# A context attention with TensorE's order staggered by one batch, late pairs weighted by ScalarE and summed by GpSimd, and two expert blocks that end without GpSimd's drain

## The chip, the cores and the metric

The kernel runs on one core of one Trainium2 chip. The metric is the time of one execution on the device, in microseconds (us); lower is better. Three runs of the kernel before are at hand, and one more with a profile, from which all rows of this text come.

## The reference

Eight sequences of 256 tokens, 256 numbers each (`x`), go through eight sublayers; four of them attend to a context `ctx` of the same shape. Only what the kernel's stages compute is kept here:

```python
x = x + L0_xattn(layernorm(x), ctx, ctx)      # 16 heads of 16      stage a0
x = x + L0_ffn(layernorm(x))                  # 16 experts choose   stage f1
x = x + L1_xattn(layernorm(x), ctx, ctx)      # 16 heads of 64      stage a2
x = x + L1_ffn(layernorm(x))                  # top 2 of 8 experts  stage f3
x = x + L2_xattn(layernorm(x), ctx)           # one head of 256     stage a4
x = x + L2_ffn(layernorm(x))                  # 8-bit weights       stage f5
x = x + L3_xattn(layernorm(x), ctx, ctx)      # 16 heads of 16      stage a6
x = x + L3_ffn(layernorm(x))                  # block quantised     in a6

def L1_ffn(x):       # every token goes to its two best experts; 4096 pairs in all
    probs = sigmoid(x @ router.T); topw, sel = top_k(probs, 2)
    topw = topw / topw.sum(-1)                # the "share" of each of the two
    return sum(topw * expert[sel](x))         # expert: relu(x @ W1)**2 @ W2

def L2_xattn(key, value):
    att = softmax(key @ value.T / sqrt(256))  # 256 x 256 for each sequence
    return att @ value                        # value is the context
```

## The kernel before

The program is seven stages, one after the other, named above. Each is a block: a list of instructions for each of the five engines (TensorE or PE, VectorE or DVE, ScalarE or ACT, GpSimd or POOL, SyncE or SP), run in the order written, with semaphores between the engines. At the end of a block every engine empties its pipeline (a `Drain`), says so on one semaphore, and goes on when all five have. There is no scheduler: the order in which the code is written is the order of the work. Each stage's GpSimd list begins with `clear_last_stage` (L92 to L94), which sets the semaphores of the last stage to zero; it consists of a `Drain` of GpSimd of its own and a clear.

**f1 to a2.** The expert-choice stage ends with four scatters (L1665), DMAs issued by GpSimd that add the last expert's rows into `x_rows` in DRAM. SP waits for the first two and loads the first half of `x` back (L1359, L1360), still in f1; the second half is loaded in a2 (L240 to L242). The first thing on GpSimd in a2 after the clear is the power that gives the first `rstd` of a layernorm (L63), then a 128x2048 copy (L591).

**f3 to a4.** The top-2 stage writes the result of every expert tile with a scatter (L2601) issued by GpSimd into `y_rows`. In a4, SP and ACT first wait until all 39 scatters have landed (L1740, L1885) and then fetch the rows back, 16 DMAs in all (`fetch_pairs`, L2803): for each token its two results, into `pair_out[:, 0]` and `pair_out[:, 1]`.

**Stage a4, `context_attention` (L1701).** `f` and `b` number the eight sequences, here called batches; a batch is two tiles of 128 tokens. The steps of a batch, with the code's names:

- DVE `take`: x += share0 * pair0 + share1 * pair1, four instructions of 128x256 (L1809)
- DVE `stats`, POOL `rstd` (L63), DVE `norm` (L70): the layernorm, result in `hn`
- PE `transpose_h` (L1760), ACT `keep_hT` (L1870): the transpose of `hn`, and its copy out of PSUM
- PE `scores` (L1769): hT times the context; two PSUM buffers in turn
- DVE `largest` (L1822), ACT `keep_prob` (L1877): the row maximum, and exp with the row sum
- PE `transpose_prob` (L1778), ACT `keep_probT` (L1883)
- PE `values` (L1787), DVE `invert` (L1827) and `add` (L1834): x += values / row sum

The tiles `hn`, `hT`, `prob`, `probT` and `nmax` exist once. In between DVE, ACT and POOL do the start of the next stage f5: `norm_stats`, `norm_x` and `norm_h` for its first 512 tokens, `dequantise`, `low_h` and `low_weights` for its first weight, with `keep_hT` and `high_weights` on ACT. SP loads the context batch by batch, each after the one before has landed.

PE's list in a4 is, after the first two: transpose_h(b+1), scores(b+1), transpose_prob(b), values(b).

## Time and profile before

| | us |
|---|---|
| median of 3 runs | 1683.46 (1682.42 to 1688.7) |
| the profiled execution | 1683.53 |
| its span, first to last instruction | 1681.7 |
| stage a4 in it, from barrier to barrier | 1222.4 to 1296.7 |
| PE busy in the span | 1415.6 (84%) |
| DVE busy | 1078.5 (64%) |
| ACT busy | 836.1 (50%) |
| POOL busy | 488.6 (29%) |

The busy shares are averages over seven stages with different limits; what counts for this change is what each engine does in stage a4 and at the two barriers. The timeline view gives start, length and engine of each instruction, and in brackets how long its engine had been idle and who released it. `PEld` is PE's loading of the stationary operand, which runs ahead of the matmuls. An engine's name with a q (`POOLq`) is its queue: waits, drains and DMA issues, which are not counted as busy.

### The profile page before, as it was taken

How to read it: one execution, taken by the hardware profiler on the slowest of the kernel's cores; microseconds unless marked ns; L12 is line 12 of the kernel's file. 1: busy time of each engine (PE TensorE's matmuls, PEld its weight loads, DVE VectorE, ACT ScalarE, POOL GpSimd, SP SyncE). 2: the span in 40 equal slices, each digit the busy share in tenths (PEclk: the TensorE clock that was granted, in tenths of full speed). 3: DMA queues.
4: the chain of work that ended last, by engine and by line, in shares of the span. 5: the costliest groups of instructions: out<-in, count | busy, mean ns of one | idle time of the engine just before them, and what ended most of it. 6: DMA issues, size and time to landing. Idle time of an engine off the chain costs nothing. (4 is left out here: it accounts for less than half of the span.)

```text
span 1681.7 us, 29336 instructions
## 1 busy us (share of the span) xinstructions
PE 1415.6 (84%) x9650; PEld 1138.7 (68%) x9650; DVE 1078.5 (64%) x2487; ACT 836.1 (50%) x1944; POOL 488.6 (29%) x428
## 2 busy tenths in 40 slices
PE   5899974999999749999999995699856897888885
PEld 4666542888888647888888873599744786555553
DVE  4677643666666537777787765644366753688886
ACT  2466541544544437666677764255423543455551
POOL 2112011577777610000000004255412311134343
PEclk8899876999999979999999997699978997799997
DMA  4322124456556345544554434122173002222110
GB/s 144 122 87 84 50 101 163 113 140 163 134 136 164 60 126 141 127 115 114 133 131 104 108 120 133 34 77 77 60 227 105 1 0 62 74 78 74 60 52 26
DMA packets 140109, 168.91 MB, mean 100 GB/s; under 512 B 20136, under 2 KB 131880, under 8 KB 137448
## 3 DMA queue, kind: packets, MB, share of 16 engines
q1 hardware_dynamic: 115000, 131.42, 26.7%
q0 software_dynamic: 16032, 27.01, 7.5%
q10 hardware_dynamic: 8976, 9.17, 1.8%
q8 instruction: 57, 0.93, 0.2%
q14 instruction: 44, 0.36, 0.1%
HBM read 75.66 MB, written 24.12 MB: 59 GB/s over the span
## 5 line engine op out<-in xcount | busy, mean ns | idle before, releaser
L1131 ACT ACTIVATE a_probT<-a_t 128x512 f32<-128x512 f32 x256 | 151.6, 602 | 164.6 <-PE a_t L860 138.5
L941 DVE TENSOR_REDUCE a_nmax<-a_s 128x2 f32<-128x512 f32 x256 | 170.9, 685 | 92.2 <-PE a_s L856 92.0
L63 POOL TENSOR_TENSOR a_rstd<-a_veps,minus_half 128x2 f32<-128x2 f32 x32 | 23.2, 724 | 507.1 <-DVE a_veps L57 507.1
L856 PE MATMUL a_s<-a_ka,a_qa 48*128 48x256 f32 x512 | 123.2, 342 | 44.8 <-DVE a_nmax L941 21.2
L856 PEld LDWEIGHTS a_s<-a_ka,a_qa 48*128 48x128 f32 x512 | 78.6, 202 | 105.3 <-issue 61.4
L441 DVE TENSOR_REDUCE a_nmax<-a_score 128x2 f32<-128x512 f32 x128 | 88.0, 687 | 86.7 <-PE a_score L334 86.6
L536 ACT ACTIVATE a_prob<-a_score,a_nmax 128x256 f32<-128x256 f32 x256 | 120.3, 481 | 34.4 <-DVE a_nmax L441 34.3
L1665 POOL DMA_INDIRECT x_rows<-f_hn,f_scatter_row x60 | 129.9, 2164 | 16.4 <-issue 16.4
L860 PE MATMUL a_t<-a_qa,a_ka 50*128 50x256 f32 x512 | 123.2, 339 | 2.2 <-DMA a_qa<-a_m_lo 1.2
L1608 ACT ACTIVATE f_gate<-f_gate 128x512 f32<-128x512 f32 x64 | 38.3, 599 | 129.0 <-PE f_gate L1411 111.0
L1521 DVE TENSOR_TENSOR f_y<-f_gate,f_value 128x512 f32<-128x512 f32 x64 | 44.0, 688 | 80.4 <-PE f_value L1411 78.4
L545 ACT COPY a_probT<-a_T 128x512 f32<-128x512 f32 x128 | 76.2, 596 | 22.7 <-PE a_T L342 21.5
L1422 PE MATMUL f_z<-area_odd_parts,f_y_hi 128*128 128x256 f32 x384 | 84.1, 286 | 0.7
L860 PEld LDWEIGHTS a_t<-a_qa,a_ka 50*128 50x128 f32 x512 | 76.9, 197 | 10.3 <-issue 5.0
L448 DVE TENSOR_SCALAR a_prob<-a_prob,a_rinv 128x256 f32<-128x256 f32 x256 | 78.9, 351 | 4.6
L333 PE MATMUL a_score<-a_k_hi,a_q 128*128 128x256 f32 x256 | 70.3, 296 | 8.7 <-DMA a_q<-a_q_fresh_lo 8.0
L342 PE MATMUL a_T<-ident,a_prob 128*128 128x128 f32 x512 | 77.0, 273 | 0.1
L876 PE MATMUL a_o<-a_probT,a_vb 128*32 128x256 f32 x1024 | 74.1, 410 | 1.1 <-ACT a_probT L1131 1.1
L1411 PE MATMUL f_gate<-f_rowsT_hi,area_odd_parts 128*128 128x512 f32 x192 | 71.2, 398 | 1.5 <-DVE f_rowsT_lo L1509 1.5
L1411 PE MATMUL f_value<-f_rowsT_hi,area_odd_parts 128*128 128x512 f32 x192 | 70.8, 396 | 0.0
L353 PE MATMUL a_o<-a_probT,a_vb 128*64 128x256 f32 x512 | 69.4, 392 | 1.2 <-ACT a_probT L545 1.2
L1658 POOL DMA_INDIRECT f_hn<-h_rows,f_gather_row x64 | 62.3, 974 | 19.1 <-issue 14.9
(385 smaller groups left out, 4414.3 us busy)
## 6 DMA issues: line engine op xcount, KB each, us to landing
area_odd<-in_L_experts SPq DMA_DIRECT2D x15, 1536.0 KB, 6.8
a_k_hi<-a_k_fresh_hi SPq DMA_DIRECT2D x128, 128.0 KB, 2.4
a_ctxT<-in_ctxT SPq DMA_DIRECT2D x64, 128.0 KB, 2.6
a_ka<-a_k_hi SPq DMA_DIRECT2D x128, 64.0 KB, 2.6
a_k_lo<-a_k_fresh_lo SPq DMA_DIRECT2D x64, 128.0 KB, 2.4
a_q<-a_q_fresh_hi SPq DMA_DIRECT2D x64, 128.0 KB, 2.4
a_q<-a_q_fresh_lo SPq DMA_DIRECT2D x64, 128.0 KB, 2.4
a_qa<-a_q_hi SPq DMA_DIRECT2D x120, 64.0 KB, 2.6
```

The source lines that it names most:

```text
L342: last = nc.tensor.transpose(ps_T[u % 2][:, kc, i, :], prob[:, u % NPROB, i, kc * P:(kc + 1) * P], chip.ident[:, :])
L441: nc.vector.tensor_reduce(nmax[:, u % NPROB, :], ps_score[u % NB][:, :, :], AX.X, ALU.max, negate=True).then_inc(sem["nmax"], 1)
L448: last = nc.vector.tensor_scalar(prob[:, u % NPROB, i, :], prob[:, u % NPROB, i, :], rinv[:, u % NPROB, i:i + 1], None, ALU.mult)
L536: last = nc.scalar.activation(prob[:, u % NPROB, i, :], ps_score[u % NB][:, i, :], ACT.Exp, bias=nmax[:, u % NPROB, i:i + 1], accum_out=rs ...
L545: nc.scalar.copy(probT[:, c % 2, :, :, qt * P:(qt + 1) * P], ps_T[u % 2][:, :, :, :]).then_inc(sem["probT"], 1)
L856: last_s = nc.tensor.matmul(ps_s[i][:, half, :], qa[rows, u % RING, j, half * P:(half + 1) * P], ka[rows, u % RING, j, :], start=True, sto ...
L860: last_t = nc.tensor.matmul(ps_t[o][:, half, :], ka[rows, v % RING, m, half * P:(half + 1) * P], qa[rows, v % RING, m, :], start=True, sto ...
L941: nc.vector.tensor_reduce(nmax[:, u % 2, :, i * PPU + j], ps_s[i][:, :, :], AX.X, ALU.max, negate=True).then_inc(sem["nmax"], 1)
L1131: nc.scalar.activation(probT[:, t % NPT, i, :, :], ps_t[i][:, :, :], ACT.Exp).then_inc(sem["exp"], 1)
L1411: last = nc.tensor.matmul(ps[f % 2][:, :], W[:, kc, f * P:(f + 1) * P], h[:, kc, :], start=(kc == 0 and i == 0), stop=(kc == KC - 1 and i ...
L1422: last = nc.tensor.matmul(ps_z[s // 2][:, s % 2, :], h[:, f, s * P:(s + 1) * P], W[:, f, :], start=(f == 0 and i == 0), stop=(f == NF - 1 ...
L1665: nc.gpsimd.indirect_dma_start(chip.x_rows, bass.IndirectOffsetOnAxis(ap=scatter_row[:, q, s:s + 1], axis=0), chip.z_last[:, s, :] if last ...
```

## The change

Three things are changed.

1. The blocks of f1 and f3 are made with `no_gpsimd_drain=True`: GpSimd no longer has a `Drain` ahead of the barrier at their end. The other engines keep theirs, and so does `clear_last_stage` at the head of the next stage. The tile of row numbers `scatter_row`, which the scatters of f1 still read, gets a place of its own for the whole program.
2. In a4, PE does transpose_prob(b), scores(b+1), transpose_h(b+2), values(b). The lists of DVE and ACT follow: ACT copies the probabilities of b, then makes those of b+1, then copies hT(b+2); DVE takes the pairs one batch earlier.
3. For batches 4 to 7 the pairs are weighted by ACT (`weigh_pairs`, four activations of 128x256 with the share as scale, in place), added to each other by POOL (`pair`, one 128x512 addition) and added to x by DVE (`take_sum`, one 128x512 addition). Batches 0 to 3 are taken as before.

PE at the start of a4, before (a_h is transpose_h, a_s scores, a_T transpose_prob, a_o values):

```order
L1760 MATMUL a_h<-ident,a_hn 128x128 x4
L1769 MATMUL a_s<-a_ctxT,a_hT 128x256 x4
L1760 MATMUL a_h<-ident,a_hn 128x128 x4
L1769 MATMUL a_s<-a_ctxT,a_hT 128x256 x4
L1778 MATMUL a_T<-ident,a_prob 128x128 x4
L1787 MATMUL a_o<-a_ctxr,a_probT 128x256 x4
L1760 MATMUL a_h<-ident,a_hn 128x128 x4
L1769 MATMUL a_s<-a_ctxT,a_hT 128x256 x4
```

and PE at the same place after:

```order
L1761 MATMUL a_h<-ident,a_hn 128x128 x4
L1770 MATMUL a_s<-a_ctxT,a_hT 128x256 x4
L1761 MATMUL a_h<-ident,a_hn 128x128 x4
L1779 MATMUL a_T<-ident,a_prob 128x128 x4
L1770 MATMUL a_s<-a_ctxT,a_hT 128x256 x4
L1761 MATMUL a_h<-ident,a_hn 128x128 x4
L1788 MATMUL a_o<-a_ctxr,a_probT 128x256 x4
L1779 MATMUL a_T<-ident,a_prob 128x128 x4
```

The transpose of the probabilities now stands ahead of the next batch's scores, and a scores or a transpose_h stands between every two steps that need a copy by ACT.

ACT after keep_hT(0) and (1), before (a_prob is keep_prob, a_probT keep_probT, a_hT keep_hT):

```order
L1877 ACTIVATE a_prob,a_rsum<-a_s,a_nmax 128x256 x2
L1883 COPY a_probT<-a_T 128x512
L1870 ACTIVATE a_hT<-a_h 128x512
L1877 ACTIVATE a_prob,a_rsum<-a_s,a_nmax 128x256 x2
L1883 COPY a_probT<-a_T 128x512
```

and after (area_even holds pair_out):

```order
L1901 ACTIVATE a_prob,a_rsum<-a_s,a_nmax 128x256 x2
L1907 COPY a_probT<-a_T 128x512
L1888 ACTIVATE area_even<-area_even 128x256 x4
L1901 ACTIVATE a_prob,a_rsum<-a_s,a_nmax 128x256 x2
L1894 ACTIVATE a_hT<-a_h 128x512
L1907 COPY a_probT<-a_T 128x512
L1888 ACTIVATE area_even<-area_even 128x256 x4
```

The weighting of a later batch's pairs stands between the copy of one batch's probabilities and the exp of the next, and the copy of hT behind that exp.

POOL in a4, before:

```order
L1900 UNCONDITIONAL_BRANCH
L94 ISA x2
L63 TENSOR_TENSOR a_rstd<-a_veps,minus_half 128x2 x5
L63 TENSOR_TENSOR f5a_rstd<-f5a_veps,minus_half 128x4
L63 TENSOR_TENSOR a_rstd<-a_veps,minus_half 128x2
```

and after:

```order
L1929 UNCONDITIONAL_BRANCH
L94 ISA x2
L63 TENSOR_TENSOR a_rstd<-a_veps,minus_half 128x2 x3
L1935 TENSOR_TENSOR area_even<-area_even 128x512
L63 TENSOR_TENSOR a_rstd<-a_veps,minus_half 128x2
L1935 TENSOR_TENSOR area_even<-area_even 128x512
L63 TENSOR_TENSOR a_rstd<-a_veps,minus_half 128x2
L1935 TENSOR_TENSOR area_even<-area_even 128x512
```

The sum of the pairs of batch f+1 stands ahead of the rstd of batch f, for f from 3 to 6.

The diff, cut to its core:

```diff
@@ f1 expert_choice_ffn
-        scatter_row = sb("scatter_row", [P, 2, SLOTS], U32)
+        scatter_row = chip.scatter_row
...
-        block = ctx.enter_context(nc.Block())
+        block = ctx.enter_context(nc.Block(no_gpsimd_drain=True))
@@ a4 context_attention, PE
             scores(0)
-            for b in range(B - 1):
-                transpose_h(b + 1)
-                scores(b + 1)
+            transpose_h(1)
+            for b in range(B):
                 transpose_prob(b)
+                if b + 1 < B:
+                    scores(b + 1)
+                if b + 2 < B:
+                    transpose_h(b + 2)
                 values(b)
                 if b == 5:
                     q.transpose_h(pe, 0)
-            transpose_prob(B - 1)
-            values(B - 1)
@@ DVE
+            def take_sum(f):
+                dve.wait_ge(sem["paired"], f - DIRECT + 1)
+                xt = chip.x[:, f * TB:(f + 1) * TB, :]
+                nc.vector.tensor_tensor(xt, xt, chip.pair_out[:, 0, f * TB:(f + 1) * TB, :], ALU.add).then_inc(sem["taken"], 1)
+                dve.wait_ge(sem["taken"], DIRECT + f + 1)
...
             largest(0)
-            for b in range(B - 2):
-                take(b + 2)
-                invert(b)
-                stats(b + 2)
+            take(2)
+            stats(2)
+            norm(2)
+            invert(0)
+            take(3)
+            for b in range(B - 1):
                 largest(b + 1)
-                norm(b + 2)
+                if b + 3 < B:
+                    stats(b + 3)
+                if b == B - 2:
+                    dve.wait_ge(sem["raw"], 16 * 4)
+                    q.dequantise(0)
                 add(b)
+                if b == B - 2:
+                    q.low_h(dve, 0)
+                invert(b + 1)
+                if b + 3 < B:
+                    norm(b + 3)
+                if b + 4 < B:
+                    take(b + 4)
@@ ACT
+            def weigh_pairs(f):
+                act.wait_ge(chip.y_back[f], 32)
+                for i in range(2):
+                    for t in range(f * TB, (f + 1) * TB):
+                        last = nc.scalar.activation(chip.pair_out[:, i, t, :], chip.pair_out[:, i, t, :], ACT.Copy, scale=chip.share[:, i, t:t + 1])
+                last.then_inc(sem["shared"], 1)
...
+            keep_hT(1)
+            keep_prob(0)
             for b in range(B):
+                keep_probT(b)
+                if b + DIRECT < B:
+                    weigh_pairs(b + DIRECT)
                 if b + 1 < B:
-                    keep_hT(b + 1)
-                keep_prob(b)
-                keep_probT(b)
+                    keep_prob(b + 1)
+                if b + 2 < B:
+                    keep_hT(b + 2)
@@ POOL
+            def pair(f):
+                pool.wait_ge(sem["shared"], f - DIRECT + 1)
+                these = slice(f * TB, (f + 1) * TB)
+                nc.gpsimd.tensor_tensor(chip.pair_out[:, 0, these, :], chip.pair_out[:, 0, these, :], chip.pair_out[:, 1, these, :], ALU.add).then_inc(sem["paired"], 1)
             for f in range(B):
+                if f >= 3 and f + 1 < B:
+                    pair(f + 1)
                 norm_rstd(nc, pool, chip, sem, nb, TB, f)
@@ f3 top2_experts
-        block = ctx.enter_context(nc.Block())
+        block = ctx.enter_context(nc.Block(no_gpsimd_drain=True))
```

## Rows read from the trace of the kernel before

**Rows 1.** Windows view, stage a4: busy us of PE, PEld, DVE, ACT, POOL; clock; DMA share, GB/s.

```profile
1222.40:1296.70 74.30, 45.38 (x200) 34.67 (x200) 52.98 (x160) 22.34 (x54) 7.96 (x10) 0.84 0.53 172
```

**Rows 2.** Source view, drains of f1 (L1288), f3 (L2154): ns min/median/max, start us.

```profile
L1288 POOLq DRAIN  x1: 13103/13103/13103, 579.9 to 579.9; - x1
...
L1288 SPq DRAIN  x1: 128/128/128, 587.8 to 587.8; - x1
...
L2154 ACTq DRAIN  x1: 401/401/401, 1214.2 to 1214.2; - x1
...
L2154 POOLq DRAIN  x1: 7655/7655/7655, 1214.6 to 1214.6; - x1
...
L94 POOLq DRAIN  x8: 55/102/147, 235.7 to 1405.0; - x8
```

**Rows 3.** Timeline at the start of a2: start us, length us, engine, line.

```profile
594.61 0.72 POOL L63 TENSOR_TENSOR a_rstd<-a_veps,minus_half 128x2 f32<-128x2 f32 x1 [6.68 <-DVE a_veps L57]
...
595.31 1.88 POOL L591 CAST area_odd_parts<-area_even 128x2048 fp32r<-128x2048 f32 x1
...
595.37 2.30 DVE L70 TENSOR_SCALAR a_hn<-x_tok,a_mv,a_rstd 128x256 f32<-128x256 f32 x2 [0.85 <-POOL a_rstd L63]
```

**Rows 4.** Timeline from f3 to a4, and the last scatters' landing (DMA view).

```profile
1214.85 0.97 POOL L2601 DMA_INDIRECT y_rows<-f_z,f_pair_row  x1 [0.58 <-ACT f_z L2548]
...
1222.64 0.88 SPq L2806 DMA_DIRECT2D area_even<-y_rows  x2
...
1230.51 0.72 POOL L63 TENSOR_TENSOR a_rstd<-a_veps,minus_half 128x2 f32<-128x2 f32 x1 [14.69 <-DVE a_veps L57]
...
y_rows<-f_z,f_pair_row POOLq DMA_INDIRECT x2, 2.4
```

**Rows 5.** One batch on PE and ACT (timeline); all of transpose_prob (source view).

```profile
1249.05 1.59 PEld L1787 LDWEIGHTS a_o<-a_ctxr,a_probT 128*128 128x128 f32 x8 [0.93 <-issue]
...
1251.52 0.60 ACT L1870 ACTIVATE a_hT<-a_h 128x512 f32<-128x512 f32 x1 [2.54 <-PE a_h L1760]
...
1252.18 1.59 PEld L1769 LDWEIGHTS a_s<-a_ctxT,a_hT 128*128 128x128 f32 x8 [0.94 <-issue]
...
1253.80 0.57 PEld L1778 LDWEIGHTS a_T<-ident,a_prob 128*128 128x128 f32 x4
...
1254.65 0.59 ACT L1883 COPY a_probT<-a_T 128x512 f32<-128x512 f32 x1 [1.62 <-PE a_T L1778]
...
1255.30 1.59 PEld L1787 LDWEIGHTS a_o<-a_ctxr,a_probT 128*128 128x128 f32 x8 [0.93 <-issue]
...
L1778 PEld LDWEIGHTS a_T<-ident,a_prob x32: 138/141/226, 1241.4 to 1290.6; 128*128 128x128 f32 x32
```

**Rows 6.** DVE and ACT in a4: one batch, and the next stage's steps (timeline).

```profile
1265.57 1.38 DVE L70 TENSOR_SCALAR f_h<-x_tok,f5a_mv,f5a_rstd 128x256 f32<-128x256 f32 x4
...
1268.91 1.79 DVE L1809 SCALAR_TENSOR_TENSOR x_tok<-area_even,x_tok 128x256 f32<-128x256 f32 x4
...
1270.82 0.73 DVE L49 BATCH_NORM_STATS2 a_stats<-x_tok 128x6 f32<-128x256 f32 x2
...
1274.35 1.38 DVE L70 TENSOR_SCALAR f_hn<-f_h,f5b_mv,f5b_rstd 128x256 f32<-128x256 f32 x4
...
1288.17 1.14 ACT L1992 CAST f_hT_hi<-f_hT 128x512 fp32r<-128x512 f32 x2
...
1291.46 1.90 ACT L1981 CAST f_W_hi<-f_W 128x2048 fp32r<-128x2048 f32 x1
...
1293.39 2.29 DVE L1962 TENSOR_TENSOR area_odd_parts<-f_W,f_W_hi 128x2048 fp32r<-128x2048 f32 x1 [2.14 <-ACT f_W_hi L1981]
```

**Rows 7.** Nearest rows to the new instructions (groups by line, mean ns).

```profile
L1237 POOL TENSOR_TENSOR x_tok<-x_tok,area_odd 128x512 f32<-128x512 f32 x8 | 10.3, 1281 | 0.2
...
L2459 DVE TENSOR_TENSOR f_sq<-f_relu 128x512 f32<-128x512 f32 x39 | 26.6, 682 | 1.6 <-ACT f_relu L2539 1.6
...
L2539 ACT ACTIVATE f_relu<-f_u,f_wide 128x256 f32<-128x256 f32 x39 | 18.3, 468 | 0.0
```

More of the change, by code:

```diff
@@ L1726, in context_attention @@
         ps_o = pb("o", [P, TB, D])
-        sem = stage_semaphores(nc, chip, stage, "stats aggr veps rstd hn hTp hT score nmax prob T probT rinv out xadd ctxT ctxr wload raw taken")
+        sem = stage_semaphores(nc, chip, stage, "stats aggr veps rstd hn hTp hT score nmax prob T probT rinv out xadd ctxT ctxr wload raw shared paired taken")
+        DIRECT = 4
         block = ctx.enter_context(nc.Block())
@@ L1798, in _ @@
                     q.transpose_h(pe, 0)
-            transpose_prob(B - 1)
-            values(B - 1)
         @block.vector
         def _(dve):
+            def take_sum(f):
[3 more added lines that the diff above has]
+                dve.wait_ge(sem["taken"], DIRECT + f + 1)
             def take(f):
+                if f >= DIRECT:
+                    take_sum(f)
+                    return
                 dve.wait_ge(chip.y_back[f], 32)
@@ L1854, in _ @@
                     q.norm_h(dve, 0)
-            invert(B - 2)
-            largest(B - 1)
-            dve.wait_ge(sem["raw"], 16 * 4)
-            q.dequantise(0)
-            add(B - 2)
-            q.low_h(dve, 0)
-            invert(B - 1)
             q.low_weights(dve, 0)
@@ L1902, in _ @@
             chip.sems.clear_last_stage(nc)
+            def pair(f):
+                pool.wait_ge(sem["shared"], f - DIRECT + 1)
+                these = slice(f * TB, (f + 1) * TB)
+                nc.gpsimd.tensor_tensor(chip.pair_out[:, 0, these, :], chip.pair_out[:, 0, these, :], chip.pair_out[:, 1, these, :], ALU.add).then_inc(sem["paired"], 1)
             for f in range(B):
+                if f >= 3 and f + 1 < B:
+                    pair(f + 1)
                 norm_rstd(nc, pool, chip, sem, nb, TB, f)
-                if f == 4:
+                if f == 5:
                     norm_rstd(nc, pool, chip, q.sa, q.na, GT, 0)
-                if f == 5:
+                if f == 6:
                     norm_rstd(nc, pool, chip, q.sem, q.nb, GT, 0)
@@ L2792, in build @@
         chip.minus_half = sb("minus_half", [P, TILES])
+        chip.scatter_row = sb("scatter_row", [P, 2, GROUPS], U32)
         area_even, even_parts = area("area_even", 9728)
```

## The prediction

> **What bounds the kernel now.** I read the windows view first. In stage a4, 74.3 us long, the busiest engine is DVE with 53.0 us, then PE with 45.4; PE's clock has a mean of 0.84 of full speed [rows 1]. No engine is full: the stage is a chain of short steps. One batch in the timeline tells which [rows 5]. PE's `values` start at 1249.05 and those of the next batch at 1255.30, a period of 6.25 us. PE's own work in it is two groups of eight matmuls, 1.62 us each from start to next start (1252.18 to 1253.80), and two of four transposes, 0.57 us each: 4.4 us. The rest are the two waits in brackets, 0.94 us ahead of `scores` and 0.93 ahead of `values`, while ACT copies hT (0.60) and probT (0.59). So in the middle of a4 PE's order sets the pace, by two exposed copies per batch.
>
> DVE is second. Its pass over one batch begins with `take` at 1268.91, and the next thing begins at 1274.35: 5.44 us, of which 1.91 are `take` and `invert` (to 1270.82) [rows 6]. Where DVE also prepares stage f5, it is DVE that sets the pace: `norm_x` alone holds it from 1265.57 to 1268.91, 3.34 us [rows 6]. From the first transpose_prob at 1241.4 [rows 5] to the stage's end at 1296.7 [rows 1] it is 55.3 us.
>
> Last the two barriers, by the rows of the drains [rows 2]. At the end of f3, ACT's drain starts at 1214.2 and takes 0.4 us; PE and DVE are done too. GpSimd's drain takes 7.66 us from 1214.6, so the barrier opens at 1222.3. The last scatter was issued at 1214.85 and scatters land 2.4 us after issue [rows 4], at 1217.25. For five microseconds nothing moves. At the end of f1 SP's drain ends at 587.9 and GpSimd's at 579.9 + 13.1 = 593.0.
>
> **The drain of f3, 5.3 us.** Without it GpSimd is at the barrier about when its last scatter has been issued (1215.8), the others by 1214.7. SP and ACT then wait for the scatters themselves, to 1217.25, and the first fetch is issued at about 1217.3 instead of 1222.64 [rows 4]. All of a4 hangs on that fetch. The gain is 5.3 us. What is late next is `clear_last_stage`, which has a drain of its own at the head of a4. With GpSimd drained before, these take 0.1 us [rows 2]; now I take it that this one waits as the removed one did, to 1222.3, since the trace shows no other reason for the wait than the scatters before it. The first use of GpSimd in a4 is the rstd at 1230.51 [rows 4], which moves to 1225.2, so 2.9 us less some 0.6 of clearing hide it. Bounds: 0 (the semaphore of the barrier waits as the drain did) and 5.3.
>
> **The drain of f1, 1.2 us.** The barrier opens at about 588.1 instead of 593.1. But in a2 GpSimd is needed at once: `stats` would be ready 5.1 us earlier, at about 589.5, while the clear's drain ends at 593.0 if it waits as the removed one did, and the clear takes some 0.3. So rstd starts at 593.4 instead of 594.61 [rows 3], and `norm`, on which PE waits, moves by the same 1.2 us. Bounds: 0 and 5.1.
>
> **PE's new order.** hT is now copied while PE does `values`, and probT while it does `scores` and `transpose_h`; both copies of 0.6 us lie beside 1.6 to 2.2 us of PE's work. PE then needs 4.4 us a batch [rows 5]. Next is DVE: its pass without `take` and `invert` is 5.44 - 1.91 = 3.5, 3.6 with `invert`; with the old `take` it would be 5.4, and the period hardly shorter than before. `take_sum` is one 128x512 addition, 0.68 us [rows 7]: 4.3 us. DVE and PE are level.
>
> What ACT and GpSimd get: four activations of 128x256 with a scale from SBUF. The nearest row, with PSUM as source, is 468 ns each [rows 7], so 1.6 to 1.9 us for four, since they overlap a little. ACT's pass becomes probT 0.5, weighting 1.7, prob 1.0, hT 0.5, in all 3.7 us, under 4.4. The path from transpose_prob over these to the next one is 0.6 + 0.6 + 1.7 + 1.0 and some semaphores, 4.2 us, also under 4.4: the cover is thin, 0.2 us. `pair` on GpSimd is 1.28 us [rows 7] and stands ahead of the rstd; `pair` starts while DVE is at `largest` and `stats`, so the rstd, due after `stats`, waits little: 0 in the walk below, 1.28 x 4 at worst.
>
> The Trainium skill, "GPSIMD Engine Reference", section Engine selection, speaks against it: an elementwise addition belongs on VectorE and is about twice as slow on GpSimd. The trace agrees, 1281 ns against 682 [rows 7]. By that rule the addition would stay on DVE and cost its pass 0.7 us more in four batches, 2.7 us; here GpSimd has the time.
>
> **The walk of a4.** From one transpose_prob to the next, after: batch 0 5.4 (DVE has two full takes, and `largest` of batch 1 is behind the second); batches 1 and 2 4.5 and 4.6 (PE 4.4, plus waits); batch 3 6.4 (DVE 4.3 and 2.0 for `norm_stats`, which is `norm_x` without its 1.38 [rows 6]); batch 4 8.1 (DVE 4.3 and 3.34 and about 0.5 of waits for rstd); batch 5 5.4 (no `take` left, 3.6 and 1.38 and waits); batch 6 4.5 (PE). The tail from the last transpose_prob is ACT and DVE alone: ACT's copies for f5, of which the row shows the second half, 1.14 [rows 6], 2.5 in all, then probT 0.5, `high_weights` 1.90, `low_weights` 2.29, `add` 0.9: 8.1. The sum is 47.0 against 55.3, 8.3 less, or 8.1 counting the barrier's 0.2. The start, to the first transpose_prob, only moves with the fetch.
>
> The walk has PE at full clock throughout, while before the stage lost some to the lower level: the mean was 0.84 [rows 1], and a load in transpose_prob took between 138 and 226 ns [rows 5]. One such stretch in the wrong place costs 1 to 2.5 us. I take 1.2 off: 6.9. Low end of this term: 8.1 - 2.5 - 2 for pairs and weights that come late, 3.6; high end 8.5.
>
> **Contention.** In a2 GpSimd's 1.88 us copy starts at 595.31 and DVE's `norm`, from 595.37, takes 2.30 us for two instructions [rows 3], where four of the same kind take 1.38 [rows 6]: DVE stood still beside GpSimd. `pair` could do this to `norm` and `take_sum`. In the walk it costs 0.2 us, since `pair` runs beside `largest`, `stats` and `add`.
>
> The Trainium skill, "SBUF — State Buffer", section Who interferes with whom, names the rule: a GpSimd instruction that reads SBUF and a DVE one with two SBUF inputs, or in a mode that uses both ports, exclude each other for a whole instruction. The row above agrees. By the rule alone, with all four additions in the way for 1.28 us, the time would be 5.1 us longer than the forecast, 1675.
>
> **Sum.** 5.3 + 1.2 + 6.9 = 13.4 us from the profiled execution's 1683.5 (its span is 1681.7, and what lies around it stays): 1670. The median of the runs is 1683.46, the same.
>
> **Rivals.**
> - *The wait vanishes with the drain.* The clear's drain finds GpSimd idle, or takes 0.1 us as in its eight rows [rows 2]; then f1 gives 5.1 instead of 1.2: 1666. Against it: all eight came when GpSimd had been drained already. 0.17.
> - *The wait stays at the barrier.* GpSimd signals only when whatever lasted to 1222.3 is over. Both barriers give nothing; only the 6.9 remain: 1676.6. For it: the trace doesn't show what GpSimd did in those 7.66 us. 0.09.
> - *Late pairs.* ACT's or GpSimd's new work, or the block of the shared access above, is late in four batches, by up to 1.3 us each: 1673 to 1675. 0.11.
> - *PE stays at the lower clock level* (slower). Scores(1) stood right behind the first matmuls, beside the table load and exp of batch 0. It now waits for transpose_prob(0), and PE idles about 3 us where it idled 0.8. If the level of 1.2 GHz then holds through a4, PE's own 4.4 us a batch become 7.2 (226/138 [rows 5]) to 8.8, and PE alone bounds all eight batches: 64 us and a tail of 3 to 4 instead of 47, some 18 more. That gives 1688, slower than before; with the barrier rival too, 1695. It decides against the change once the low level holds for more than two thirds of the stage. Against it: in the new order PE is busier, and the level was up for most of a stage in which it was less busy. 0.03.
>
> **How the numbers follow.** The forecast's own case has 0.60. The range reaches from 1683.5 - 5.3 - 5.1 - 8.5 = 1664.6 to 1683.5 - 5.3 - 3.6 = 1674.6: 1664 to 1675, and holds 0.83. Half a percent is 8.4 us, about what a measurement of this kernel can tell from no change. Faster by more (under 1675): forecast, the first rival, most of late pairs, 0.87. Within: 0.11. Slower by more (over 1692): 0.02.
>
> **What would show it.** Right: the first fetch of pairs 2.5 us after the last scatter's issue; a drain of several us at L94 at the head of a2 and a4; a period of 4.5 us between transposes of batches 1 to 3; no idle time of PE behind ACT's copies; from the first transpose_prob to the end of a4 47 to 49 us. Wrong: L94's drains stay at 0.1 us; GpSimd's barrier semaphore still at 1222; PE's rows of `scores` at twice their length in the middle of the stage; DVE's `norm` at 1 to 2 us beside `pair`; ACT's weighting above 2 us for four.

## The result and the profile after

In 13 runs each the changed kernel takes 1678.2 us at the median (1668.4 to 1683.1) and the kernel before 1685.8 (1681.0 to 1699.4). The medians are 7.6 us apart; the ratio of all runs is 0.9936, 95% interval 0.9918 to 0.9954, which is 10.8 us: faster, by 0.5 to 0.8%. The forecast was 1670 us, with a range of 1664 to 1675, and a gain of 13.4 us. The median lies outside the range.

The profiled execution of the changed kernel took 1680.07 us, its span 1678.3. Its stages, against those of the profiled execution before:

| stage | before, us | after, us | difference |
|---|---|---|---|
| a0 | 235.6 | 235.4 | -0.2 |
| f1 | 357.5 | 355.0 | -2.5 |
| a2 | 420.9 | 420.5 | -0.4 |
| f3 | 208.4 | 199.9 | -8.5 |
| a4 | 74.2 | 69.8 | -4.4 |
| f5 | 108.3 | 108.2 | -0.1 |
| a6 | 276.7 | 289.4 | +12.7 |

Up to the end of f5 the change gains 16.1 us, more than forecast. Then a6, a stage that the change doesn't touch, gives 12.7 back. The windows view of the kernel before, f1 and a6 (busy us of PE, PEld, DVE, ACT, POOL; clock; DMA share, GB/s):

```profile
235.60:593.10 357.50, 309.68 (x1730) 263.60 (x1730) 219.53 (x400) 151.78 (x228) 217.60 (x164) 0.93 0.54 140
...
1404.90:1681.60 276.70, 212.02 (x1636) 148.05 (x1636) 204.92 (x443) 122.44 (x261) 93.75 (x96) 0.88 0.21 64
```

and of the changed kernel, f1, a4 (the answer to [rows 1]), a4 from the first transpose_prob, and a6:

```profile
235.40:590.40 355.00, 312.33 (x1730) 264.07 (x1730) 219.42 (x400) 151.77 (x228) 217.50 (x164) 0.94 0.53 139
...
1210.80:1280.60 69.80, 44.65 (x200) 35.74 (x200) 49.44 (x148) 28.74 (x70) 13.66 (x15) 0.80 0.57 187
1232.64:1280.60 47.96, 38.93 (x184) 31.64 (x184) 38.72 (x113) 25.24 (x63) 11.17 (x12) 0.91 0.46 155
1388.80:1678.20 289.40, 224.69 (x1636) 156.61 (x1636) 204.47 (x443) 122.59 (x261) 93.76 (x96) 0.83 0.20 62
```

Two things are to be seen. In a6 all engines do the same work, but PE's granted clock has a mean of 0.83 instead of 0.88, and PE is busy for 12.7 us more. In f1 PE is busy for 2.65 us more at a clock that is no lower: something in the change makes PE slower there.

**The drains.** Source view of the changed kernel: f1's block (L1288), f3's (L2190) and the clear (L94), against [rows 2].

```profile
L1288 POOLq EVENT_SEMAPHORE  x2: 17/17/17, 590.3 to 590.4; - x2
...
L1288 SPq DRAIN  x1: 131/131/131, 590.1 to 590.1; - x1
...
L2190 POOLq EVENT_SEMAPHORE  x2: 17/17/17, 1210.7 to 1210.8; - x2
...
L2190 ACTq DRAIN  x1: 403/403/403, 1210.2 to 1210.2; - x1
...
L94 POOLq DRAIN  x8: 59/107/1028, 235.6 to 1388.9; - x8
```

The timelines of the two stage starts, against [rows 3, 4]:

```profile
588.21 1.97 POOL L1665 DMA_INDIRECT x_rows<-area_odd,scatter_row  x1 [0.30 <-issue]
...
591.86 0.73 POOL L63 TENSOR_TENSOR a_rstd<-a_veps,minus_half 128x2 f32<-128x2 f32 x1 [1.67 <-DVE a_veps L57]
...
592.62 2.30 DVE L70 TENSOR_SCALAR a_hn<-x_tok,a_mv,a_rstd 128x256 f32<-128x256 f32 x2 [0.85 <-POOL a_rstd L63]
...
1210.88 0.97 POOL L2637 DMA_INDIRECT y_rows<-f_z,f_pair_row  x1 [0.59 <-POOLq L2190]
1213.44 0.87 SPq L2843 DMA_DIRECT2D area_even<-y_rows  x2
...
1221.48 0.72 POOL L63 TENSOR_TENSOR a_rstd<-a_veps,minus_half 128x2 f32<-128x2 f32 x1 [9.63 <-DVE a_veps L57]
```

Both barriers open as soon as the other engines are there. In f3 GpSimd has signalled at 1210.7 and its last scatter is carried out at 1210.88: without the drain its queue runs ahead of its own work. From the last scatter to the fetch it is 2.56 us instead of 7.79. In f1 the barrier opens 2.2 us after the last scatter's issue instead of 7.1. And the clear's own drains take 0.1 us in a2 and 1.03 at most: the removed wait has not moved into them. The first rstd of a2 starts 1.5 us after the barrier, as before (594.61 after 593.1).

**The new order.** Timeline of the changed kernel in the middle of a4, against [rows 5]:

```profile
1232.64 1.12 PE L1779 MATMUL a_T<-ident,a_prob 128*128 128x128 f32 x4 [3.02 <-ACT a_prob L1901]
...
1233.55 3.62 PE L1770 MATMUL a_s<-a_ctxT,a_hT 128*128 128x256 f32 x8
...
1239.99 1.89 PE L1770 MATMUL a_s<-a_ctxT,a_hT 128*128 128x256 f32 x8
...
1244.08 0.66 PE L1779 MATMUL a_T<-ident,a_prob 128*128 128x128 f32 x4
...
1245.26 1.70 ACT L1888 ACTIVATE area_even<-area_even 128x256 f32<-128x256 f32 x4
...
1245.92 0.68 DVE L1809 TENSOR_TENSOR x_tok<-x_tok,area_even 128x512 f32<-128x512 f32 x1
...
1247.04 1.27 POOL L1935 TENSOR_TENSOR area_even<-area_even 128x512 f32<-128x512 f32 x1 [2.14 <-ACT area_even L1888]
...
1247.30 0.74 DVE L49 BATCH_NORM_STATS2 a_stats<-x_tok 128x6 f32<-128x256 f32 x2
...
1248.58 0.60 PE L1779 MATMUL a_T<-ident,a_prob 128*128 128x128 f32 x4
...
1249.94 0.74 DVE L70 TENSOR_SCALAR a_hn<-x_tok,a_mv,a_rstd 128x256 f32<-128x256 f32 x2
...
1254.39 1.26 POOL L1935 TENSOR_TENSOR area_even<-area_even 128x512 f32<-128x512 f32 x1
...
1254.90 0.76 DVE L57 TENSOR_TENSOR a_veps<-a_veps,a_mv 128x2 f32<-128x2 f32 x1
...
1255.03 0.66 PE L1779 MATMUL a_T<-ident,a_prob 128*128 128x128 f32 x4 [1.88 <-ACT a_prob L1901]
```

The first row is transpose_prob(0), ahead of which PE stood idle for 3.02 us, the second is scores(1), the third scores(2). From scores(1) on PE's rows have no bracket up to the transpose_prob at 1255.03: it goes from one step to the next without a wait, 4.50 us a batch. Then come the two batches in which DVE prepares the next stage, and PE waits again, 1.88 us here. scores(1) takes 3.62 us where the same eight matmuls take 1.89 in the next batch: PE runs them at the lower of its two clock levels, 1.2 GHz. Windows view of the stretch of scores(1) and of scores(2), with granted clocks of 0.50 and 1.00:

```profile
1232.70:1236.80 4.10, 4.10 (x12) 3.44 (x13) 2.47 (x7) 2.19 (x5) 1.28 (x2) 0.50 0.46 142
1240.10:1241.80 1.70, 1.70 (x10) 1.33 (x9) 1.60 (x6) 1.61 (x4) 0.00 (x0) 1.00 0.72 189
```

From transpose to transpose it is 6.9, 4.5, 4.5, 6.5, 8.1, 5.4, 4.2 and a tail of 7.9, in all 48.0 us; the walk said 5.4, 4.5, 4.6, 6.4, 8.1, 5.4, 4.5 and 8.1. The new instructions cost what the rows foretold: 1.70 us for four activations, 1.27 for GpSimd's addition, 0.68 for DVE's, and DVE's `stats` beside GpSimd is as short as ever. One row of DVE is not: the small addition `a_veps`, 128x2 with both inputs in SBUF, takes 0.16 us seven times and 0.76 once, beside the last of GpSimd's additions, and ends with it (1255.66 and 1255.65). It does so in each of the 14 profiles of kernels with these additions.

### The profile page after: what moved, and what is told of

Same layout as the page of the kernel before. It is cut to its first block and busy times, and to the rows that moved or that the text cites. A ratio compares the mean times of both kernels' runs of the same rounds, so it can differ in the third digit from the quotient of the medians.

```text
span 1678.3 us, 29353 instructions
## 1 busy us (share of the span) xinstructions
PE 1422.7 (85%) x9650; PEld 1142.5 (68%) x9650; DVE 1072.9 (64%) x2475; ACT 843.1 (50%) x1960; POOL 493.3 (29%) x432
## 5 line engine op out<-in xcount | busy, mean ns | idle before, releaser
L1665 POOL DMA_INDIRECT x_rows<-f_hn,scatter_row x60 | 129.5, 2159 | 16.4 <-issue 16.4
```

The source lines that it names most:

```text
L1665: nc.gpsimd.indirect_dma_start(chip.x_rows, bass.IndirectOffsetOnAxis(ap=scatter_row[:, q, s:s + 1], axis=0), chip.z_last[:, s, :] if last ...
```

## The experiments

The runs of one kernel scatter by 15 us and more, in step with their mean granted clock: the 13 of the changed kernel go from 1668.4 us at 0.921 to 1683.1 at 0.907. A straight line through all runs, with one level for each kernel, has a slope of 1.2 us for each 0.001. So the table gives the mean, the mean clock, and the mean brought to a clock of 0.915 by this slope, mean + 1200 x (clock - 0.915). A single run typically lies 2.3 us off the line, so the error of a level is 0.2 us for the kernel before and 0.5 to 0.9 for the others. Three runs of the kernel before, whose clock fell under 0.89, are left out, and so are its first 13, of which no clock is on record. The last column takes the clock as something that comes from outside; where a change itself moves the clock, the plain mean is what counts. e11 ran once only, for its profile.

| kernel | runs | mean, us | clock | at 0.915 |
|---|---|---|---|---|
| before (all runs with a clock) | 139 | 1686.8 | 0.9160 | 1688.0 |
| changed (the first 13 and e3) | 25 | 1676.0 | 0.9136 | 1674.3 |
| e1 drains only | 12 | 1681.2 | 0.9159 | 1682.3 |
| e2 a4 only | 12 | 1683.4 | 0.9145 | 1682.8 |
| e5 pad only | 10 | 1687.9 | 0.9146 | 1687.4 |
| e6 scatter_row behind | 7 | 1675.3 | 0.9113 | 1670.9 |
| e7 stagger only | 10 | 1674.4 | 0.9168 | 1676.6 |
| e8 pairs only | 10 | 1681.2 | 0.9169 | 1683.5 |
| e9 and e17 six batches' pairs | 18 | 1672.6 | 0.9144 | 1671.9 |
| e10 plain drain | 10 | 1682.5 | 0.9104 | 1677.0 |
| e12 e6 with f1's drain | 10 | 1678.5 | 0.9128 | 1675.9 |
| e13 e9 with one addition | 8 | 1673.0 | 0.9141 | 1671.9 |
| e14 e9 with two | 12 | 1674.5 | 0.9147 | 1674.1 |
| e15 and e18 e9 with three | 14 | 1668.4 | 0.9189 | 1673.1 |
| e16 before with two | 12 | 1689.8 | 0.9163 | 1691.4 |

### Each half alone, and both kernels again (e1 to e4)

e1 keeps the stage a4 of before and drops both drains:

```diff
-        block = ctx.enter_context(nc.Block())
+        block = ctx.enter_context(nc.Block(no_gpsimd_drain=True))
```

> Both barriers without GpSimd's drain, stage a4 in the old order. If each part's gain is local and the parts add: the barrier of f1 opens 5.1 us sooner after the last scatter's issue (2.1 us instead of 7.1), the first fetch of a4 comes 2.6 us after the last scatter's issue instead of 7.8, GpSimd's drain at the head of a2 and a4 takes about 0.1 and 1 us, a4 lasts from first transpose of probabilities to its end 55.3 us as before, and the median is 10 us under that of the kernel before. If the drain's wait only moves: 1 to 5 us. If the lower TensorE clock in stage a6 (289.4 us there instead of 276.7) is brought about by stages that start earlier, a6 is long here too and the median is near that of the kernel before; if it comes and goes from one execution to the next whatever the kernel, a6 lies anywhere between 276 and 290 us.

e2 is the kernel before with the new `context_attention`:

```diff
-            for b in range(B - 1):
-                transpose_h(b + 1)
-                scores(b + 1)
+            for b in range(B):
                 transpose_prob(b)
+                if b + 1 < B:
+                    scores(b + 1)
```

> The new stage a4 alone, both drains kept. If the parts add: from the first transpose of probabilities to a4's end 48 us as in the changed kernel instead of 55.3, all other stages as before, and the median 7 us under that of the kernel before. If the busier a4 is what costs clock later (TensorE is given less in a6 because it was busier in a4), a6 lasts 289 us again with a granted clock of 0.83, and the median is 5 us above that of the kernel before. If a6's clock is a matter of the single execution, a6 lies anywhere between 276 and 290.

e3 is the changed kernel and e4 the kernel before, unedited.

> The changed kernel once more. If the change itself lowers the clock in a6: a6 289 us and clock 0.83 again. If single executions differ: a6 anywhere between 276 and 290, and the spans of the runs follow their mean clock, about 1 us for each 0.001; at the same mean clock as a run of the kernel before it is 12 to 17 us shorter.

> The kernel before once more, for its stage lengths in a second execution. If single executions differ in a6's clock, a6 is not 276.7 us here but up to 290; if a6's clock belongs to the kernel, it is 276 to 278 us with 0.88.

Measured: ratio 0.9958 (0.9928 to 0.9987) for e1, 0.9982 (0.9953 to 1.0011) for e2, 0.9927 (0.9899 to 0.9954) for e3, 0.9991 for e4. At equal clock the drains give 5.7 us, a4 5.2, both 13.7. The halves add up to 10.9 (error 1), 2.8 under the whole; the rows don't show this gap (7.7 us by the barriers and f1 for e1, 6.5 by a4 in e2), and what it is stays open. Both halves gave less than expected by their medians, 7.5 and 3.3 us where 10 and 7 had been written down. In the traces: the barrier of e1's f1 opens 2.1 us after the last scatter, the fetch comes 2.56 us after it; from the first transpose_prob e2 needs 48.75 us and e3 47.1, the kernel before (e4) 54.9 and e1 54.8. The long a6 is not the change's own: the kernel before has it too in its second profile, and the changed kernel has a shorter one; e1 had 280.7 us and e2 289.6. Windows view of e4, a6:

```profile
1402.70:1692.10 289.40, 224.20 (x1636) 155.84 (x1636) 205.05 (x443) 122.44 (x261) 93.85 (x96) 0.83 0.20 62
```

and of e3, a6:

```profile
1389.90:1670.50 280.60, 214.10 (x1636) 149.40 (x1636) 204.30 (x443) 122.31 (x261) 93.72 (x96) 0.86 0.21 64
```

So a6's clock differs between executions of one kernel, and that is 13 us between the first and the second profile of the kernel before. But f1 showed a loss that is steady: 352.8, 352.7 and 353.4 us from its barrier to the last scatter's issue in the three kernels without the drain, 350.4, 350.1 and 349.1 in the three with it.

### Where f1 loses 2.6 us (e5, e6, e11)

`scatter_row`, 32 bytes of each partition, was moved out of f1 to a place ahead of the two large areas that hold weights. e5 only adds such a gap to the kernel before:

```diff
+        chip.pad = sb("pad", [P, 2, GROUPS], U32)
         area_even, even_parts = area("area_even", 9728)
```

> The kernel before with 32 bytes per partition, never used, ahead of the two large areas in SBUF: only addresses change. In the three kernels without the drain, f1 took 352.8, 352.7 and 353.4 us from its barrier to its last scatter's issue, in the three with it 350.4, 350.1 and 349.1. If the place of scatter_row, which moves both areas by 32 bytes, is the cause: 352.5 to 353.5 us here, and TensorE's groups of gate and value in f1 start 1.40 us apart instead of 1.375. If the missing drain is the cause, or single executions differ: 349 to 350.5 and 1.375.

e6 is the changed kernel with the tile behind the areas:

```diff
-        chip.scatter_row = sb("scatter_row", [P, 2, GROUPS], U32)
         area_even, even_parts = area("area_even", 9728)
         area_odd, odd_parts = area("area_odd", 12288 + 500)
+        chip.scatter_row = sb("scatter_row", [P, 2, GROUPS], U32)
```

> The changed kernel with scatter_row allocated behind the two large areas instead of ahead of them, so that the areas lie where they lay before. If addresses are the cause of f1's loss: f1 takes 350 us to its last scatter's issue, with the barrier 2.1 us behind that issue as in the changed kernel, and the median is 2.5 us under that of the changed kernel at the same mean clock. If the missing drain is the cause: 353 us again and no change.

e11 is the changed kernel with a hole in f1:

```diff
         scatter_row = chip.scatter_row
+        hole = sb("hole", [P, 12, 2], U32)
```

> The changed kernel with 96 unused bytes in f1 where scatter_row was: the tiles of f1 behind it lie 96 bytes further, so that the two areas and these tiles stand 64 bytes apart from their old relation instead of 32. If only the odd 32 bytes hurt: gate and value groups 1.373 us apart in f1 and 350 us to the last scatter's issue. If any shift against each other hurts: 1.400 and 353 us.

Windows view, f1, of e5 and of e6:

```profile
233.20:589.60 356.40, 308.78 (x1730) 262.84 (x1730) 219.55 (x400) 151.88 (x228) 217.54 (x164) 0.93 0.53 140
```

```profile
230.60:582.90 352.30, 309.48 (x1730) 263.12 (x1730) 219.55 (x400) 151.89 (x228) 217.59 (x164) 0.94 0.53 140
```

e6 has PE's 309.5 us back, f1 takes 352.3 us, and at equal clock the kernel is 3.4 us faster than the changed one (error 1; the plain means differ by 0.7, since the seven runs of e6 had a low clock). My reason was half wrong: e5 moves the areas as well and loses nothing (349.4 us to the last scatter's issue, groups mostly 1.373 us apart). What differs: e5 moves f1's own tiles behind the gap along with the areas, the changed kernel moves the areas alone, since its gap ahead of them is made up by the tile that f1 no longer has. e11, 64 bytes apart instead of 32, loses too: 352.0 us, and 311.6 us of PE. So the place of PE's two operands relative to each other sets how fast these matmuls run. Of the 127 distances between groups in f1, the one met most often is 1.373 us in the 13 profiles without the shift and 1.39 to 1.40 in the 7 with it; over all groups the mean goes from 1.38 to 1.39 or 1.40, some 1%. Which pairs of addresses hurt, and why, stays open.

### Which part of a4 gives what (e7, e8)

e7 lets DVE take all pairs itself, in the new order:

```diff
-        DIRECT = 4
+        DIRECT = B
```

> The changed kernel with DVE taking all eight batches' pairs itself (no weighting on ACT, no addition on GpSimd): TensorE's new order alone. If DVE is next behind TensorE, as the prediction has it: transposes of probabilities 5.4 us apart where they are 4.5 in the changed kernel, and 50 to 52 us from the first to a4's end instead of 48. If DVE's pass is covered: 48 us as in the changed kernel.

e8 has the old order, with the late pairs on ACT and GpSimd:

```diff
                 keep_prob(b)
                 keep_probT(b)
+                if b + DIRECT < B:
+                    weigh_pairs(b + DIRECT)
```

> The changed kernel with TensorE's old order, but the late pairs weighted by ACT and added by GpSimd. If the two exposed copies set the pace in the middle of a4: 6.2 us from transpose to transpose as before, gains only where DVE prepares the next stage (batches 3 and 4, about 1 us each), and 52 to 54 us to a4's end instead of 55.3. If DVE had set the pace all along: 48 to 50 us.

Timeline, transposes of probabilities, of e7

```profile
1231.45 0.60 PE L1779 MATMUL a_T<-ident,a_prob 128*128 128x128 f32 x4
...
1237.08 0.66 PE L1779 MATMUL a_T<-ident,a_prob 128*128 128x128 f32 x4 [1.10 <-ACT a_prob L1901]
...
1242.39 0.65 PE L1779 MATMUL a_T<-ident,a_prob 128*128 128x128 f32 x4 [0.65 <-ACT a_prob L1901]
```

and of e8

```profile
1241.22 0.60 PE L1779 MATMUL a_T<-ident,a_prob 128*128 128x128 f32 x4
...
1247.48 0.60 PE L1779 MATMUL a_T<-ident,a_prob 128*128 128x128 f32 x4
```

In e7 the period is 5.6 and 5.3 us, PE waits for `prob`, and behind that for DVE; 51.05 us to a4's end, at a clock of 0.88 there. In e8 it stays at 6.26, and the whole is 54.6. As forecast: the order alone gives 4 of the 7 to 8 us, moving the pairs alone next to nothing (0.2 us less than e1), both together 7 to 8. At equal clock, against e1, the order alone gives 5.7 of 8.0 us and the pairs alone cost 1.2 (error 1). The second bottleneck is worth money only when the first is gone. e8's bounds, 52 to 54, were a bit too hopeful: with DVE's shorter pass batches 3 and 4 take 7.6 and 9.8 us where e1 has 7.8 and 9.6. Here GpSimd's additions hold `a_veps` twice, for 0.96 and 0.95 us.

### The wait is the plain drain's (e10, e12)

e10 puts a drain on GpSimd at the head of a2 and a4:

```diff
+            nc.gpsimd.drain()
             chip.sems.clear_last_stage(nc)
```

> The changed kernel with a drain on GpSimd of the same plain kind as the removed ones ahead of the clear at the head of a2 and of a4. If the removed wait belongs to the plain drain: it lasts until 7.1 us after the last scatter's issue here too, so 4.9 us at the head of a2, where the first rstd then starts 4 us later than in the changed kernel; at the head of a4 until 1218, with no effect, since GpSimd is first needed 10.6 us after that issue. Cost 4 us. If it belongs to the place ahead of the barrier: 0.1 and 1 us, as the clear's drain, and no cost.

e12 is e6 with f1's drain kept:

```diff
-        block = ctx.enter_context(nc.Block(no_gpsimd_drain=True))
+        block = ctx.enter_context(nc.Block(no_gpsimd_drain=False))
```

> The version with scatter_row behind the areas, with f1's drain kept. By the rows of the barriers it costs 5.1 us: f1 357.3 us from barrier to barrier instead of 352.3, everything else the same, and at the same mean clock 5 us more than that version. If the next stage hid most of it, as the prediction had it: 1.2 us.

Source view and timeline of e10, its drain in a2 (L588), in a4 (L1932), and a2's first rstd:

```profile
L588 POOLq DRAIN  x1: 4698/4698/4698, 582.1 to 582.1; - x1
...
L1932 POOLq DRAIN  x1: 7405/7405/7405, 1207.1 to 1207.1; - x1
...
587.26 0.72 POOL L63 TENSOR_TENSOR a_rstd<-a_veps,minus_half 128x2 f32<-128x2 f32 x1 [5.40 <-issue]
```

The plain drain waits as the removed ones did, 4.7 and 7.4 us, at the end of a stage and at the head of the next; the clear's doesn't. Why the plain one lasts that long, when the scatters land 2.4 us after their issue, stays open. In a2 it moves rstd from 1.5 to 5.3 us after the barrier: the cost is 3.8 us there (2.7 at equal clock, error 1), in a4 nothing (69.1 us). e12 takes 357.5 us for f1 against e6's 352.3, and at equal clock 5.0 us more in all. So f1's drain was worth its full 5.1 us, not 1.2.

### A version beyond the change (e9), and a6's start (e13 to e18)

e9 is e6 with the pairs of six batches weighted by ACT:

```diff
-        DIRECT = 4
+        DIRECT = 2
@@ ACT
             keep_hT(0)
+            weigh_pairs(2)
+            weigh_pairs(3)
             keep_hT(1)
```

> The changed kernel with scatter_row behind the areas, and with ACT weighting six batches' pairs instead of four: those of batches 2 and 3 right after the first copy of hT, where ACT waits 4.8 us in the changed kernel, GpSimd's two additions after the second rstd. If DVE's take of batches 2 and 3 (1.8 us each, now 0.7) holds the first period: 5 us from the first transpose of probabilities to the second instead of 6.1, and 46 us to a4's end instead of 47.1, the median 1 us under that of the version with scatter_row behind the areas. If the pairs of batches 2 and 3 land too late: the copy of hT(1) moves back and the first transpose comes later than 19.2 us after the fetch.

Ratio 0.9923 (0.9898 to 0.9949), again 0.9914 in e17. Its first period is 6.07 us as in e3 and e6, not 5: ACT and GpSimd are in time, but DVE wasn't what held it. Timeline of e9, scores(1) and DVE's `largest` of batch 1:

```profile
1223.39 3.11 PE L1770 MATMUL a_s<-a_ctxT,a_hT 128*128 128x256 f32 x8
...
1226.61 0.69 DVE L1833 TENSOR_REDUCE a_nmax<-a_s 128x2 f32<-128x512 f32 x1 [2.71 <-PE a_s L1770]
```

DVE had been waiting for scores(1) for 2.71 us. In all 14 profiles with the new order PE idles 3.0 us ahead of the first transpose_prob, scores(1) takes 2.8 to 3.6 us, and `largest` waits for it; in the six with the old order PE idles 0.2 to 0.3 us there and scores(1) takes 2.0. In the changed kernel's first profile `largest` waits 1.43 us, which is nearly the whole of the first period's excess, 6.9 for 5.4. scores(0) ran at the lower level in both orders (3.4 to 3.8 us); in the old one the level is up by scores(1), in the new one only after it. So the new order starts with a price: an idle stretch, and one more batch of scores at the lower level. A second such scores, that of batch 6 with 3.3 to 3.6 us, stands behind the other idle stretch of 3.3 us in e2, e11, e12, e14 and e15, and those are, besides e7, the ones that take 48.5 us or more from the first transpose_prob; in the old order batch 6 has it in five of six profiles. No run tried to fill the idle stretches. e9 takes 47.1 us to a4's end, as without the two more batches; its first addition on GpSimd stands beside `norm` of batch 1, which takes 1.70 us for its two instructions instead of 0.74. The gain over the changed kernel is that of the place of `scatter_row`.

What was left was a6. Kernels with the full new a4 ran at a mean clock of 0.913, the kernel before at 0.916, which is some 3 us given back. In nine profiles of such kernels a6 took 280.6 to 289.8 us, mean 287.4. e13, e14 and e15 put a pause ahead of a6's barrier, with one, two and three additions; e16 does it to the kernel before:

```diff
             for g in range(GROUPS):
                 group(g)
+            for k in range(3):
+                nc.vector.tensor_tensor(q.W[1][:, 2 * k:2 * k + 2, :], y[:, 1, :], y[:, 1, :], ALU.add)
```

> The version of e9 (six batches' pairs weighted by ACT, scatter_row behind the areas) with one extra 128x512 addition of DVE, 0.7 us, at the end of f5, so that a6 starts 0.7 us later. If a6's length follows the place at which it starts: a6 280 to 284 us instead of the 288 of e9, mean clock 0.916 or more, and a median 1 to 4 us under that of e9 in spite of the pause. If a6's clock is a matter of the single execution: the mean of the runs 0.7 us above that of e9, within 2 us, and a clock of 0.9145 within 0.0012.

> The same with two additions, 1.3 us. If a6's length follows its start: another length again, the same in its profile as its runs' mean says, with a jump of 5 us or more against one of the neighbours. If not: the mean 1.3 us above that of e9, within 2 us.

> The same with three additions, 1.9 us. If a6's length follows its start: as for the two others. If not: the mean 1.9 us above that of e9, within 2 us.

> The kernel before with two such additions at the end of f5, 1.3 us. In the kernel before a6 took 276.7 and 289.4 us in two profiles. If its start decides: the mean clock falls from 0.916 to 0.914 or under, and the mean time grows by 3 us or more. If not: 1.3 us more, within 2 us, at 0.916.

In the profiles a6 took 278.1, 283.6 and 277.3 us, and 284.4 in e16. The means of e13 and e14, 0.1 and 1.6 us above e9's, are what was written down for "if not"; e15's was 3.3 us lower than e9's, outside it. In e13 and e15 the profiled execution was the fastest of its eight, so its a6 doesn't stand for the others. So e9 and e15 ran once more, side by side:

> The version of e9 once more. If a6's length follows its start: a6 285 to 290 us in the profile, mean clock 0.914 or less, mean time 3 us or more above that of the run with the pause beside it. If not: as the run beside it, less 1.9 us.

> The version of e15 once more, three extra additions at the end of f5. If a6's length follows its start: a6 277 to 280 us in the profile again, mean clock 0.917, mean time 3 us or more under that of the run without a pause. If the low time of e15 was chance: 1.9 us above the run without a pause, within 2 us.

Ratios 0.9914 (0.9883 to 0.9944) and 0.9885 (0.9848 to 0.9922). Windows view, a6, of e17

```profile
1382.10:1670.30 288.20, 223.41 (x1636) 155.79 (x1636) 204.70 (x443) 122.56 (x261) 93.80 (x96) 0.84 0.19 62
```

of e15

```profile
1380.90:1658.20 277.30, 212.61 (x1636) 148.64 (x1636) 204.67 (x443) 122.22 (x261) 93.77 (x96) 0.88 0.21 64
```

and of e18

```profile
1381.30:1664.20 282.90, 217.90 (x1636) 152.05 (x1636) 204.70 (x443) 122.21 (x261) 93.75 (x96) 0.85 0.21 63
```

e17's a6 is within its bounds, e18's, 282.9 us, is not (277 to 280 was expected). Side by side e18's mean is 5.1 us under e17's, with an error of 3.7. Together: 1668.4 us with the pause (14 runs, error 1.7), 1672.6 without (18 runs, error 1.1), 4.2 us less with an error of 2.0; and a6 took 277.3 to 283.6 us in all four profiles with a pause against 287.4 at the mean without. Against this stand e13 and e14, which show nothing in their means, and e16, 1.5 us above the runs of the kernel before beside it, which is the pause and no more. The pause of three additions was repeated because it had come out low, and the eight runs by which it was chosen are part of its mean. So that a6's length depends on the moment at which it starts is possible, and not shown.

## Why the prediction was wrong

- **The level, 1683.5 us: the step that failed first.** "The median of the runs is 1683.46, the same" took three runs and one profile for the kernel's level, which is 1686.8 over 139. With that base and the mechanisms as forecast the time would have been 1673.4.
- **f3's drain, 5.3 us: right.** 7.79 to 2.56 us from scatter to fetch is 5.2.
- **f1's drain, 1.2 us: wrong in two ways that partly cancel.** The step of the mechanism that failed is "I take it that this one waits as the removed one did". The rival that had 0.17 was true: the wait vanishes with the drain, and the barrier gives 5.1 us (e12: 5.0). I had taken two instructions of one name for one thing; the eight rows of 0.1 us [rows 2] were the better witness than my argument against them. The sum also had no term for the tile that moves, and gave no reason for that: it costs 2.6 us in f1 (e6). Net 2.5. That this lies near the forecast is luck.
- **The walk, 6.9 us: right, somewhat low.** 48.0 instead of 55.3 is 7.3, and 47.1 in five other profiles (47.7 to 48.75 in the rest) is 8.2, the value before the allowance of 1.2 for the clock. The only period off by over 0.4 us is the first, 6.9 for 5.4, and the reason given for it, DVE's two full takes, is not what set it: PE's scores(1) ran at the lower level, 3.62 us instead of 1.9, as it does in every profile with the new order (e9). The allowance was for such a stretch "in the wrong place"; here is one, and it comes with the order.
- **Contention, 0.2 us, and late pairs: right in size, with one wait left out.** `norm`, `take_sum` and `stats` went on undisturbed. But GpSimd's last addition holds the small `a_veps` for 0.6 us. The trace agrees here with the Trainium skill, "SBUF — State Buffer", section Who interferes with whom, by which a GpSimd instruction that reads SBUF and a DVE one with two SBUF inputs exclude each other: `a_veps` has two such inputs, `stats` has one. It costs little, since DVE meets it once; that period took 6.5 us where 6.4 were forecast.
- **PE at the lower level through a4: did not come.** The clock had a mean of 0.91 from the first transpose on. What this rival built on did come, 3.02 us of idle PE in place of the 0.8, and then the lower level for one batch. Its sum doesn't close either: 64 and 3 to 4 less 47 is 20 to 21 us, not 18. The stage whose clock mattered most was a6, which no rival named.
- **The sum.** By rows the change is worth 5.2 + 2.5 + 7.3 to 8.2, that is 15 to 16 us; at equal clock the runs show 13.7 (error 0.5), the forecast 13.4. From the forecast to the mean of the changed kernel's 25 runs it is 3.3 us for the level, 0.3 off for the gain, and 2.9 for a mean clock of 0.9136 instead of 0.9160: 1676.0. The lower clock is a term that the sum put at nothing, and its cause is open. The other 2.2 us to 1678.2 come from which 13 runs were taken: the twelve of e3 have a median of 1674.2, which lies inside the range. The range had terms for the mechanisms alone, none for executions that differ by 15 us with the clock, though the three runs shown already spread by 6. Wider by 5 us on each side it holds both medians.

## What to carry to other kernels

Before a time is forecast, ask how far two executions of the unchanged kernel lie apart, stage by stage; here one untouched stage moved by 13 us, as much as the whole change gave, and only runs compared at the same clock showed the parts. A copy of ACT between two steps of PE is hidden by putting another batch's step between them, and it pays to lighten the second engine in the same change: here the order alone gave half to seven tenths, the lighter engine alone nothing. Look too at how long TensorE is idle at the new order's start, and at how long its next rows are. A tile that is moved moves its neighbours: look at PE's busy time in every stage afterwards, also where no instruction was changed.

## What the runs showed of the hardware

- A plain drain of GpSimd ends 6.9 to 7.4 us after the issue of the last scatter, though scatters land 2.4 us after issue; a drain that goes with the clearing of a range took 0.1 us in a2 and 1.03 in a4, where it stood right behind a scatter.
- Without the drain, GpSimd's queue signals the barrier (1210.7) before its engine has taken up the last scatter (1210.88).
- Groups of 128x512 matmuls in f1 most often started 1.373 us apart or 1.39 to 1.40, with PE busy for 308.3 to 309.7 us or 311.6 to 313.0, by the relative place of their operands in SBUF alone, in each of the 20 profiles.
- A 128x2 addition of DVE with both inputs in SBUF took 0.76 us instead of 0.16 beside GpSimd's 128x512 addition and ended with it; `stats`, with one input, kept its 0.74.
- Behind 3.02 us of idle PE in a4, eight matmuls took 2.8 to 3.6 us in 14 profiles; behind 0.3 us, 2.0 in the six others.
- TensorE's mean clock in one and the same stage was 0.83 to 0.88 in different executions, 276.7 to 289.8 us. PE had been idle for 5.8 us at the stage's start in the changed kernel's profile and in that of the kernel before alike; the mean clock of the first 70 us is 0.63 in one and 0.73 in the other, and 0.89 and 0.93 in the rest.
